# A graph layer's segment sums: one loop for all rounds, level 2 in two row groups, bounds counted in the middle, and the last step's edges in two transfers

## The reference, cut to what matters

```python
agg = jax.ops.segment_sum(edge_attr, col, num_segments=x.shape[0])   # col = dst, sorted
h = jnp.concatenate([x, agg, u[batch]], axis=1)                      # batch is all zeros
h = jax.nn.relu(h @ W1 + b1)
x = _layernorm(x + (h @ W2 + b2), axis=-1)                           # no gain, no shift
```

## Time and profile before

| | before |
|---|---|
| runs | 280.07, 281.10, 281.37 us; median 281.1 us |
| profiled execution | 281.48 us, of which the span is 279.8 us |
| DMA in the span | 110.06 MB, mean 393 GB/s |
| busy PE / DVE / ACT / POOL | 77% / 60% / 18% / 15% |

### The profile page before, as it was taken

How to read it: one execution, slowest core, us unless ns; L and a number is a source line. 1 busy time by engine, 2 the same in 40 slices (tenths; PEclk the granted TensorE clock), 3 DMA queues, 4 the chain that set the end, 5 groups by cost and what they waited for, 6 DMA issues and landing times.

```text
span 279.8 us, 15302 instructions
## 1 busy us (share of the span) xinstructions
PE 214.5 (77%) x6767; PEld 169.0 (60%) x6767; DVE 167.7 (60%) x425; ACT 51.3 (18%) x100; POOL 40.8 (15%) x49
## 2 busy tenths in 40 slices
PE   0988599986786696696867499898867867767982
PEld 0866487755665575575545378677655655655761
DVE  7932375774665655754854426958565563797552
ACT  0511031311220220221200211322221121120210
POOL 6400020220300400400401100303020030021020
PEclk9986899999999999999997869999999999997998
DMA  7999999999999999999999999999999999999991
GB/s 249 351 387 399 401 399 401 401 400 401 402 399 403 401 400 402 401 401 412 417 411 414 414 401 406 418 417 418 413 418 415 418 416 414 411 418 413 413 396 62
DMA packets 30623, 110.06 MB, mean 393 GB/s; under 512 B 1976, under 2 KB 3150, under 8 KB 30606
## 3 DMA queue, kind: packets, MB, share of 16 engines
q1 hardware_dynamic: 27508, 105.83, 95.3%
q10 hardware_dynamic: 3098, 4.00, 4.1%
HBM read 106.63 MB, written 3.20 MB: 393 GB/s over the span
## 4 chain that ended last, share of the span: by engine, by line
PE 62%; issue 17%; DMA 13%; DVE 5%; POOL 1%; ACT 1%; DVEq 0%; POOLq 0%; ACTq 0%
PE rows_ps L808 33%; PE cols_ps L820 15%; DMA slots<-in_edge_attr 13%; PE hid_ps L852 4%; PE hid_ps L834 3%; PE hid_ps L843 2%; PE hid_ps L828 1%; ACT rows L416 1%; DVE first_of_pair L538 1%; POOL rstd L380 1%; DVE dst_local L548 1%; DVE stats L628 1%; PE rows_ps L967 1%; DVE z L643 0%; DVE agg_t L606 0%
## 5 line engine op out<-in xcount | busy, mean ns | idle before, releaser
L808 PE MATMUL rows_ps<-slots,hot 64*32 64x128 f32 x6240 | 113.3, 285 | 38.4 <-issue 36.4
L808 PEld LDWEIGHTS rows_ps<-slots,hot 64*32 64x32 f32 x6240 | 93.8, 110 | 57.1 <-issue 55.1
L606 DVE TENSOR_TENSOR agg_t<-agg_t,cols_ps 128x128 f32 (+1 forms) x65 | 21.7, 333 | 99.4 <-PE cols_ps L820 99.3
L820 PE MATMUL cols_ps<-row_hot,rows 128*128 128x128 f32 (+1 forms) x260 | 56.2, 340 | 13.3 <-ACT rows L416 5.7
L580 DVE TENSOR_TENSOR hot<-edge_node,iota 128x768 f32<-128x768 f32 x65 | 62.0, 954 | 2.3 <-issue 2.1
L416 ACT ACTIVATE rows<-rows_ps 128x256 f32<-128x256 f32 x65 | 24.9, 383 | 182.6 <-PE rows_ps L808 178.6
L820 PEld LDWEIGHTS cols_ps<-row_hot,rows 128*128 128x128 f32 x260 | 40.4, 196 | 27.2 <-issue 15.2
L380 POOL TENSOR_TENSOR rstd<-var_eps,minus_half 128x4 f32<-128x4 f32 (+1 forms) x13 | 16.6, 1274 | 204.0 <-DVE var_eps L637 204.0
L596 DVE TENSOR_TENSOR row_hot<-row_node,iota 128x256 f32<-128x256 f32 (+1 forms) x65 | 37.6, 578 | 0.0
L371 POOL TENSOR_TENSOR z<-x_rows,b_all 128x512 f32<-128x512 f32 (+1 forms) x13 | 16.5, 1272 | 29.1 <-PE hid_ps L828 29.1
L643 DVE TENSOR_SCALAR z<-z,moments,rstd (+1 forms) x49 | 17.6, 418 | 0.9 <-POOL rstd L380 0.9
(11 more groups left out here) (111 smaller groups left out, 64.8 us busy)
## 6 DMA issues: line engine op xcount, KB each, us to landing
slots<-in_edge_attr SPq DMA_DIRECT2D x65, 1536.0 KB, 17.8
x_rows<-in_x ACTq DMA_DIRECT2D x11, 256.0 KB
out<-z SPq DMA_DIRECT2D x11, 256.0 KB
dst_int<-in_dst SPq DMA_DIRECT2D x1, 384.0 KB, 4.2
dst_int<-in_dst ACTq DMA_DIRECT2D x1, 384.0 KB, 4.6
x_rows<-in_x ACTq DMA_DIRECT2D x1, 192.0 KB
out<-z SPq DMA_DIRECT2D x1, 192.0 KB
rest_slot<-in_edge_attr ACTq DMA_DIRECT2D x1, 160.0 KB, 9.1
```

Source lines behind the costliest of these rows:

```text
L606: V.tensor_tensor(cols, cols, cols_ps[:, 0:n], ALU.add).then_inc(added, 1)
L808: done = T.matmul(rows_ps[i][c * SPAN:(c + 1) * SPAN, h, 0:feats], hot[j][part, c * RUN + r, :], slots[part, j, c, r * feats:(r + 1) * fea ...
L820: done = T.matmul(cols_ps[:, 0:n], rows[i][:, h, :], row_hot[j][:, h, 0:n], start=(h == 0), stop=(h == HALVES - 1))
```

## The change

- **One loop.** Sparse and dense laps become one `one_lap`, on TensorE and on VectorE. In every lap level 2 of step t follows level 1 of step t. One pair of `rows_ps` and `rows` is left of three.
- **Level 2 in two row groups.** Rows 0 to 63 and rows 64 to 127 of the partial sums get windows of their own, each 128 nodes wide, with a base of its own. A step's level 2 is four matmuls of 64 rows where it was two of 128, and VectorE adds twice where it added once; it reads ten bases a lap instead of five.
- **Where the products stand.** Of a lap's TensorE work for the blocks, the agg product stands behind level 1 of the lap's step 0, the second product behind that of step 1, the transposes of x behind that of step 2, the x product behind that of step 3.
- **b2 by TensorE.** A product of a row of ones and b2, 512 columns wide (`bias2`), opens the bank of the second product ahead of level 1 of each lap's last step. GpSimd's addition goes; x is loaded into `z` itself and ScalarE copies it from there into `x_rows` (`stage_x`).
- **Blocks moved by 128 nodes.** The last block is nodes 0 to 127 and the others lie above it in whole blocks of 512, so the odd one is the first (490 nodes) and no longer the last but one. Its loads and its store are three transfers each, in the first lap and at the first store.
- **Bounds in the middle.** `judge` is in lap 6, the sum of counts and the plan in lap 7; the 320 edges of the rest are summed there too and no longer in lap 0. The matmuls of 384 columns in lap 12 are gone.
- **The last step's edges in two transfers.** Step 64 is loaded as two transfers of packets of 1536 bytes, three of a partition's six edge rows each. TensorE waits for the second half between the third and the fourth round of level 1.
- **At the start.** The weights are asked for in another order, x before them and behind a memset of `z`; step 0's indices come in packets of 24 bytes instead of 48.

```diff
...
-COLS = 224
-DENSE_COLS = 128
+COLS = 128
...
-SETS = (0, 1, 0, 1, 2)
-DENSE_LAP = 6
-DENSE = DENSE_LAP * LAP
+DENSE = 6 * LAP
+
+JUDGE = 6
...
             def load(t):
-                if t >= DENSE:
+                if t == held:
+
+                    for part, landed in ((slice(0, RUN // 2 * feats), edges_in[t % SLOTS]), (slice(RUN // 2 * feats, RUN * feats), half_in)):
+                        sp.dma_start(slots[:, t % SLOTS, :, part], edge_steps[0][:, :, part]).then_inc(landed, 16)
+                elif t >= DENSE:
...
+            G.memset(z[:, 0, :, :], 0.0).then_inc(z_zero, 1)
+            G.memset(z[:, final, :, :], 0.0).then_inc(z_zero, 1)
...
-                G.tensor_tensor(z[:, bass.ds(i, 1), 0:m, :].rearrange("p o r f -> p (o r) f"), x_rows[:, 0:m, :],
-                                b2_all[:, :].unsqueeze(1).broadcast_to([P, m, feats]), ALU.add).then_inc(z_ready, 1)
...
             def copy_rows(t):
-                i = SETS[t % LAP]
                 act.wait_ge(level1_done, t + 1)
-                if t >= 2:
-
-                    act.wait_ge(level2_done, t - 1)
-                A.activation(rows[i][:, :, :], rows_ps[i][:, :, 0:feats], ACT.Copy).then_inc(rows_copied, 1)
+                if t:
+
+                    act.wait_ge(level2_done, t)
+                A.activation(rows[:, :, :], rows_ps[:, :, 0:feats], ACT.Copy).then_inc(rows_copied, 1)
...
+            def stage_x(seq):
+
                 i = seq % places
...
+                act.wait_ge(x_in, x_landed(seq // places, i))
+                A.activation(x_rows[:, :, :], z[:, i, :, :], ACT.Copy).then_inc(x_staged, 1)
...
+            def add(t, at):
                 dve.wait_ge(level2_done, t + 1)
...
+                for g in range(GROUPS):
+
+                    dve.wait_ge(added, t * GROUPS + (g + 1))
+                    cols = agg_t[:, bass.ds(at[g], COLS)]
+                    V.tensor_tensor(cols, cols, cols_ps[:, g, 0:COLS], ALU.add).then_inc(added, 1)
...
                 for r in range(RUN):
+                    if j == LAP - 1 and r == RUN // 2:
+
+                        pe.wait_ge(ids_copied, SHARE)
+                        pe.wait_ge(half_in, lap * 16 + 16)
...
                 for h in range(HALVES):
-                    done = T.matmul(cols_ps[:, 0:n], rows[i][:, h, :], row_hot[j][:, h, 0:n], start=(h == 0), stop=(h == HALVES - 1))
+                    for g in range(GROUPS):
+                        part = slice(g * HALF, (g + 1) * HALF)
+                        done = T.matmul(cols_ps[:, g, 0:COLS], rows[part, h, :], row_hot[j][part, h, :], start=(h == 0), stop=(h == HALVES - 1),
+                                        tile_position=(g * HALF, 0))
...
+                T.matmul(y_bank[:, 0:n], ones[0:1, :], b2_rows[:, :, :].rearrange("a r f -> a (r f)")[:, 0:n], start=True, stop=False)
...
                     t = lap * LAP + j
+                    if j == 4:
+                        bias2(lap, ROWS)
                     level1(t, lap, j)
...
```

More of the change, by code:

```diff
@@ L154, in residual_gnn_layer @@
         row_hot = [sb(f"row_hot{i}", [P, HALVES, COLS]) for i in range(HOTS)]
-        rows = [sb(f"rows{i}", [P, HALVES, feats]) for i in range(3)]
+        rows = sb("rows", [P, HALVES, feats])
         agg_t = sb("agg_t", [P, width])
@@ L526, in _ @@
             V.memset(cap[:, 0, :], float(nodes - 1))
-            V.memset(cap[:, laps - 1, :], float(FIRST - DENSE_COLS))
             dve.wait_ge(part_made, 1)
@@ L684, in sparse_lap @@
                     t = lap * LAP + j
-                    mixed = not isinstance(lap, int) and j + AHEAD >= LAP
-                    add(t, at[j], False)
+                    add(t, at[j * GROUPS:(j + 1) * GROUPS])
                     if not isinstance(lap, int):
-                        if j == 2:
+                        if j == 1:
                             residual(lap - 1, lap - 1)
+                            with dve.If(lap == JUDGE):
+                                make_rest_hot()
+                                judge()
+                        elif j == 2:
+                            variance(lap - 1, lap - 1)
+                            with dve.If(lap == JUDGE + 1):
+                                make_plan()
+                                add_rest(t)
@@ L738, in _ @@
-            with dve.Fori(DENSE_LAP, laps) as lap:
-                dense_lap(lap)
+            V.tensor_copy(edge_node[:, held, :, :], first_int[:, :, :])
+            with dve.Fori(1, laps) as lap:
+                one_lap(lap)
             residual(final, final)
@@ L844, in product1_agg, with bias2 @@
-                done.then_inc(hid_done, 1)
-            def start_of(i):
-                return 0 if isinstance(i, int) and i == final else (blocks - 1) * BLOCK - i * BLOCK
+                n = rows_of(i) * P
+                T.matmul(hid_ps[:, 0:n], w1a[:, :], agg_t[:, bass.ds(at, n)], start=False, stop=True).then_inc(hid_done, 1)
+            def bias2(seq, m):
+                pe.wait_ge(row_node_made, GROUPS)
+                pe.wait_ge(b2_made, 1)
+                pe.wait_ge(z_made, seq + 1)
+                n = m * feats
+                T.matmul(y_bank[:, 0:n], ones[0:1, :], b2_rows[:, :, :].rearrange("a r f -> a (r f)")[:, 0:n], start=True, stop=False)
```

458 lines of the change are left out of this document (179 added, 279 removed).

## The result

| | before | changed |
|---|---|---|
| median | 280.1 us (278.8 to 281.6, 22 runs) | 281.94 us (279.99 to 285.73, 22 runs) |
| ratio | | 1.0052, 95% interval 1.003 to 1.0074 |
| profiled execution | 281.48 us, span 279.8 | 283.43 us, span 281.6 |

The change is slower by 0.5%, where 278.5 us was forecast and 281.3 was the range's upper end. It also scatters twice as widely, 5.7 us against 2.8. (A ratio leaves out executions over 1.5% above the kernel's fastest; the medians include them, so the two need not agree.)

What follows compares the result with a forecast made beforehand. DMA was taken to bound the middle, landings and tail the end: step 63 lands at 263.0, last level 1 ends 269.05, plus 5.30 and 0.45 gives 274.8, plus 2.06 span 276.9, time 278.5 us; range 276.7 to 281.3.

Steps and rivals of the forecast that it cites:

- costs at nothing: Each lap: one row-buffer pair, stage_x and five more base registers hide behind slot waits; TensorE lap 18.2 us, DMA 19.4.
- The start: Program start: x pieces, memset and 512 packets of 24 bytes beside loads cost between -0.3 and +0.4 us, taken as 0.
- The span behind the last store: Program end: from the last store's issue to the end of the span, 2.06 us, the same as before.
- Code: Instruction fetches: one loop leaves four or five, none after lap 0; step 63 lands 1.6 us earlier (between 0 and 1.7).
- TensorE behind step 63: From step 63's landing at 263.0: level 1, x product, level 2 (0.6), b2 (1.05); step 64's level 1 ends at 269.05.
- the tail: Last level 1 to last store's issue: 5.30 us plus 0.45 for a second addition and longer level 2.
- the split hidden: Step 64's load: second half lands 0.6 us later, at 267.3, but TensorE is busy until then, so the split buys nothing.
- The base: Starting point: profiled execution of 281.48 us, TensorE 2.5 us late at step 64's level 1 from laps 11 and 12.
- The slow engine: Rival: another fetch keeps one DMA engine late, step 63 lands at 264.6 again, 280.1 us; chance 0.2.
- The stores: Rival: blocks' stores drain at the end, the last store queues behind them, 0.7 us more, 279.2; chance 0.14.
- half clock at the end: Rival: TensorE at 1.2 GHz from step 63 to the end, 6.8 us more, 285.3; chance 0.06.
- DMA shows gaps in the middle: Sign of a wrong forecast: waits for level 1 so long that DMA runs dry mid-kernel; no size given.

Runs made afterwards that it cites:

- e2: The change with only lap 0's x product and b2 product moved to lap 1: 281.64 us, ratio 1.0056.
- e9: The change with GpSimd's second batch of memsets of agg_t held until VectorE has made base_diag: 281.5 us, ratio 1.0041.
- e15: e1 with e9's wait, split of step 64 and order at the start kept as in the change: 280.45 us, ratio 1.0008.
- e11: The change with VectorE made to wait for GpSimd's last memset of agg_t ahead of base_diag: 283.94 us, ratio 1.0127.
- e12: The kernel before with VectorE made to wait for GpSimd's last memset of agg_t ahead of base_diag: 279.98 us, ratio 0.9991.
- e1: The change with each lap's x and b2 products moved into the next lap, the final block's 128 columns wide: 281.95 us, again 281.36.
- e4: The change with three unused matmuls of 512 columns as TensorE's first work: 283.61 us, ratio 1.0058.
- e13: e10 without the general path's branch and code, the plan's flag still read: 279.44 us, ratio 0.9987.
- e10: e1 with step 64 in one transfer of 6144-byte packets, ScalarE's first transfers in the old order, GpSimd's second memsets behind base_diag: 280.31 us, ratio 0.9992.
- e16: The kernel before, unchanged, profiled once more: one run, 279.59 us.
- e17: The kernel before without the three matmuls of 384 columns ahead of the last level 1s: 279.26 us, ratio 0.9951.
- e5: The kernel before with four unused matmuls of 512 columns more in lap 0: 281.34 us, ratio 1.0037.

## Why the prediction was wrong, point by point

- **The step that failed: costs at nothing.** "Hide behind waits for slots, as long as a lap of TensorE is shorter than a lap of DMA" was worked out for a later lap at the full clock, with a full queue. Lap 0 has neither: five slots, cold code and the low level's durations. Two products of 2.07 us there, and level 2 waiting for ScalarE's copy in the same step, helped to push the end of level 1 of step 4 from 36.1 to 44.0 us, past what the queue could bridge. The profiled execution lost 2.8 us by it. How much of it is the products' own isn't shown: e2, without them in lap 0, gains nothing in the median, e9 has them and no hole, and e15's gain of 0.9 us over e9 has the shorter tail in it. What e11 and e12 do show is that lap 0 of the change has no slack left for a late start, and that of the kernel before has.
- **The start, taken at 0 within -0.3 and +0.4.** The order of the transfers was within that. What was missed is, first, that level 1 of step 0 starts 1.3 us later; 1.0 of it are two small products for the bias, at 12.77 and 13.28 us, which stood behind that level 1 before. Second, the instruction that makes `base_diag` comes into GpSimd's memsets, and with lap 0's slack gone a late start reaches the end: 2.0 us of median when forced (e11 against the change), 0 before (e12). That it makes the unforced change's executions of 284 to 286 us is inferred: the profiles with 3.41 are of e1, e2 and e4, at 284 to 286 us. e9's median is 0.4 lower than the change's, and none of its 12 executions is above 283.31.
- **The span behind the last store: 2.06 became 3.5** (3.2 in e9). In the profiles of the new loop it is 2.8 to 3.5 us, in those of the old one 1.9 to 2.1. The forecast took this term over from before as it was, and it grew by 0.8 to 1.4. Seen beside it: at the very end the last store's packets take longer to trickle out. DMA in 40 slices of 0.12 us from 276.8 us, before and changed:

```profile
GB/s 0 0 0 0 137 0 0 0 0 0 0 0 0 0 4 209 256 77 0 0 68 0 0 0 0 0 0 0 0 0 0 0 0 0 0 0 0 0 0 0
```

```profile
GB/s 68 68 34 51 17 34 154 0 0 0 0 0 0 0 0 0 0 0 239 248 60 0 68 9 26 17 9 9 0 0 0 0 0 0 0 0 0 0 0 0
```

  Before, the store is out in 0.5 us, and one packet of the instruction queue q14 (the 68) comes after it. Changed, two come with it, and the last of its packets follow up to 0.7 us later. In e11 and e13 only one comes with the store, and the span ends 2.8 and 3.0 us behind the issue, the two shortest of the new loop; in the others two come and it is 3.2 to 3.5. That these fetches hold the store up fits, but no run was made to take both away.
- **Code, -1.6 at the landing: half right.** q8 has 6 packets and no second group: four in lap 0, and one at 277.5 us, where the kernel before has one as well. But the sixth is a late fetch, at 200.4 us in the change, at 62 to 64 in e9 and e10. With the hole out and no fetch between 64 us and the last landing, step 63 landed at 263.6 (e9: 246.2 and 17.4), 1.0 and 0.6 us ahead of the two profiles of before; forecast 263.0. In e15, whose late fetch came at 184 us, it landed at 265.8 (249.9 and 15.9); 0.5 us or so of that is a hole from 49 to 63 us (376 and 392 GB/s). The change, with a hole of 2.8 us and a late fetch, landed 2.8 behind e9. So what one late fetch costs isn't settled; the new loop has not got rid of it, only moved it.
- **TensorE behind step 63 and the tail: right** to 0.1 us each from the landing on, as the rows above show: level 2 in eight instructions 0.71 (0.6 taken, 0.44 to 0.9 bounded), the b2 product 1.05 until level 1 starts (1.05), the split hidden. In e9 the landing, the end of the last level 1 and the last issue are at 263.6, 269.50 and 275.2, each within 0.6 us of the forecast's 263.0, 269.05 and 274.8; with the longer end the execution took 280.21.
- **The base.** The sum stood against an execution of 281.48 us in which a dip of the clock in lap 12 had put the last level 1 1.8 us later than e16. The forecast laid TensorE's 2.5 us of lateness there to the extra work of laps 11 and 12; e16, with the same work and without the dip, is 1.0 us late (268.0 to 269.03). Of the 3.4 us that were to be won there, 1.8 were to be had only in executions with that dip; the median of before over 22 runs is 280.1, and the sum's 3.0 us of gain stood against 281.48. The part that was real, the 384-column matmuls, e17 has for itself: 0.5%.
- **The rivals.** The slow engine came true in so far as a late fetch stayed, but the landing was later than its 264.6. The stores were not it: their packets end at 277.6 us, half a microsecond ahead of the last store's issue. Nor was half clock at the end: the last two level 1s take 1.58 and 1.59 us. "DMA shows gaps in the middle" stood in the list of what would prove it wrong, without a price.

Open: what keeps e5 0.4% slower, how often the change draws the late start, what the two products in lap 0 cost by themselves, what a late fetch costs, and what holds the end 0.8 to 1.4 us longer.

## What to carry to other kernels

A stage that is hidden in steady state must be priced once more for the first lap, with its own clock, its own fetches and the few buffers that are then out: slack is per lap, not per kernel. When a kernel's executions scatter more than those of its neighbour, look at more than one profile; a bad one and a good one differ in one row. And before counting a gain against a profile, check in a second profile that its last wait is there too.

## What the runs showed of the hardware

- A VectorE instruction that meets a batch of eight GpSimd memsets gets in either behind the first (0.50 us) or behind all (3.41 us), with the same start to 10 ns in the profile; alone it takes 0.29 (e9).
- TensorE's first level 1 lasts 2.81 us, as at the low level, though the granted clock is 1.00 in the window 14:21 of the change. In e4, behind 5.5 us of matmuls at the start, it lasts 2.81 too, there at a granted clock of 0.50.
- The first lap's code comes in 16 KB packets 6 to 8 us apart beside a full DMA (about 19, 25, 33 and 41 us in the changed kernel), and TensorE stands up to 2.9 us for one.
